# Edge counts in blocks of 16 destinations, the first residual bias as a matmul, and the last row tiles one by one

## The reference, cut to what matters

```python
n = 1250                                   # nodes, 768 features; 41250 edges, sorted by destination
loop = arange(n); dst = concat([edge_index[1], loop]); src = concat([edge_index[0], loop])
# layer 0: graph convolution
deg = segment_sum(ones, dst); norm = rsqrt(deg)[src] * rsqrt(deg)[dst]
x = layernorm(x + segment_sum((x @ W)[src] * norm[:, None], dst) + b)
# layer 1: two attention layers
def gat_conv(x, W, a_src, a_dst, bias, heads):
    xl = (x @ W).reshape(n, heads, -1)
    e = leaky_relu((xl * a_src).sum(-1)[src] + (xl * a_dst).sum(-1)[dst], 0.2)
    e = exp(e - segment_max(e, dst)[dst])
    alpha = e / segment_sum(e, dst)[dst]
    return segment_sum(xl[src] * alpha[..., None], dst).reshape(n, -1) + bias
h = gat_conv(x, W1, a_src1, a_dst1, b1, 4)                       # 4 heads of 256
h1 = relu(layer_norm(h, g1, be1)) + (x @ Wr1 + br1)              # "r1" is x @ Wr1 + br1
h = gat_conv(h1, W2, a_src2, a_dst2, b2, 1)
out = layernorm(x + layer_norm(h, g2, be2) + (h1 @ Wr2 + br2))
```

## Time and profile before

| what | us |
|---|---|
| three runs: lowest, median, highest | 953.65, 956.11, 956.56 |
| the profiled execution's own time | 956.15 |
| its span in the profile | 954.3 |
| PE, VectorE, ScalarE, GpSimd busy in the span | 852.7, 710.2, 300.8, 82.6 |

### The profile page before, as it was taken

How to read it: one execution, slowest core, us unless ns; L and a number is a source line. 1 busy time by engine, 2 the same in 40 slices (tenths; PEclk the granted TensorE clock), 3 DMA queues, 4 the chain that set the end, 5 groups by cost and what they waited for, 6 DMA issues and landing times.

```text
span 954.3 us, 12872 instructions
## 1 busy us (share of the span) xinstructions
PE 852.7 (89%) x4906; PEld 545.5 (57%) x4906; DVE 710.2 (74%) x1088; ACT 300.8 (32%) x451; POOL 82.6 (9%) x82
## 2 busy tenths in 40 slices
PE   2899999799799989965999988769899999999994
PEld 2566665466555434422888876658555656655552
DVE  6688888777746659794666698886796588965667
ACT  3133233500012101113577756635212207740000
POOL 2000000200000004441000010000110000000011
PEclk8899999899999989997999997889999999999998
DMA  7000001214121221313230011220102443222222
GB/s 274 1 1 1 2 1 67 84 40 156 75 121 45 67 79 67 121 66 94 91 105 28 28 50 56 67 71 23 45 27 96 157 179 101 84 83 67 67 68 95
DMA packets 23253, 70.32 MB, mean 74 GB/s; under 512 B 2614, under 2 KB 3338, under 8 KB 23070
## 3 DMA queue, kind: packets, MB, share of 16 engines
q1 hardware_dynamic: 21326, 61.80, 18.7%
q0 software_dynamic: 1872, 7.78, 2.4%
HBM read 49.26 MB, written 20.31 MB: 73 GB/s over the span
## 4 chain that ended last, share of the span: by engine, by line
issue 32%; PE 23%; DVE 21%; POOL 3%; ACT 2%; DMA 2%; POOLq 0%; DVEq 0%; ACTq 0%; SPq 0%
PE psum L787 12%; PE psum L608 9%; DVE arena L1186 7%; DVE arena L1287 2%; DVE arena L1291 2%; DVE arena L1310 1%; POOL arena L558 1%; DVE arena L1154 1%; ACT arena L922 1%; DMA arena<-as_scratch 1%; ACT arena L934 1%; DVE arena L1196 1%; POOL arena L542 1%; DVE arena L1318 1%; DVE arena L1181 1%
## 5 line engine op out<-in xcount | busy, mean ns | idle before, releaser
L608 PE MATMUL psum<-arena 128*128 128x512 f16 (+1 forms) x1080 | 227.6, 369 | 10.2 <-DVE arena L1006 9.2
L787 PE MATMUL psum<-arena 128*128 128x257 f32 x800 | 188.5, 399 | 31.1 <-ACT arena L922 22.1
L854 ACT ACTIVATE arena<-psum 128x320 f16<-128x320 f32 (+7 forms) x146 | 86.7, 629 | 380.6 <-PE psum L608 124.9
L787 PEld LDWEIGHTS psum<-arena 128*128 128x128 f32 x800 | 159.1, 200 | 59.0 <-issue 24.4
L608 PEld LDWEIGHTS psum<-arena 128*128 128x128 f16 (+1 forms) x1080 | 104.9, 99 | 118.1 <-DVE arena L1006 9.4
L760 PE MATMUL psum<-arena 128*128 128x512 f16 x960 | 159.3, 328 | 3.0 <-ACT arena L922 2.4
L760 PEld LDWEIGHTS psum<-arena 128*128 128x128 f16 x960 | 94.3, 98 | 65.8 <-ACT arena L922 2.8
L934 ACT ACTIVATE arena<-arena 128x640 f32<-128x640 f32 x160 | 119.6, 830 | 8.1 <-DVE arena L1291 7.0
L1186 DVE CUSTOM_DVE_ANT_0 arena<-arena 128x1280 bf16<-128x1280 bf16 x50 | 88.1, 1826 | 15.6 <-DMA arena<-as_scratch 11.8
L847 PE MATMUL psum<-arena 128*128 128x512 f16 x600 | 98.4, 326 | 0.0
L1287 DVE TENSOR_TENSOR arena<-arena 128x640 f32<-128x640 f32 x80 | 66.4, 830 | 37.0 <-ACT arena L934 36.2
(11 more groups left out here) (151 smaller groups left out, 608.5 us busy)
## 6 DMA issues: line engine op xcount, KB each, us to landing
arena<-in_L_gnn_W_dram SPq DMA_DIRECT2D x14, 384.0 KB, 5.7
r_scratch<-arena SPq DMA_DIRECT2D x10, 512.0 KB, 2.6
arena<-uv_scratch SPq DMA_DIRECT2D x16, 320.0 KB, 3.8
arena<-r_scratch SPq DMA_DIRECT2D x10, 512.0 KB, 3.6
x_scratch<-arena SPq DMA_DIRECT2D x10, 384.0 KB, 4.4
arena<-x_scratch SPq DMA_DIRECT2D x10, 384.0 KB, 3.6
r_scratch<-arena SPq DMA_DIRECT2D x10, 384.0 KB, 2.6
arena<-r_scratch SPq DMA_DIRECT2D x10, 384.0 KB, 4.0
```

The costliest lines, as they stand in the source:

```text
L608: ins = pe.matmul(o[:, a:b], part[:, k, ds(t * P, P)], w[:, k, a:b], start=(k == 0 and n == 0 and m == 0), stop=(k == kn - 1 and n == 1))
L787: last = pe.matmul(p_att[:, j, 0:HID + 1], pf[n % PSLOTS][:, j * P:(j + 1) * P], xl[ch % H][:, k, 0:HID + 1], start=(k == 0), stop=(k == T ...
L854: act.activation(out_, in_, ACT.Copy, scale=scale).then_inc(signal, 1)
```

## The change

Three edits are joined, and each is visible in the order of the instructions.

*Counting.* A block is 16 destinations, so there are 80 blocks, and a group is 6 edge tiles (one group per block, as with 32 and 10 before). The ring has 4 slots, PSUM 3. First and last edge tile of a block are packed in one word, read with one register load and taken apart by two register operations. The keys have two buffers and are shifted four blocks before they are wanted. x @ W is cut into 60 pieces that are spread over the blocks (`pieces_until`), none ahead of the first block; the six low parts of W0 come one by one between blocks 2 to 7. TAIL is 1.

*First residual.* The bias is split in two float16 rows (high and low part) and added by two matmuls of 512 columns that open each tile's sum. GpSimd makes the split once; its ten adds are gone, and ScalarE's output is stored as it is. The transposes of the sums and of the shifts stand inside the product's queue. ScalarE starts the exponentials before it takes the last tile out of PSUM.

*End.* Three pairs, then four single tiles. Of the last tile PE sums columns 512 to 768 first and then 0 to 512, VectorE takes the two parts as they come, and scales and stores in two halves.

```diff
-WD = 32
+WD = 16
-G = 10
+G = 6
+KSLOTS, CSLOTS = 4, 3
-TAIL = 3
+TAIL = 1
+PACK = 10
+W_LAG = 2
+def pieces_until(b):
+    return max(0, min(b + 1 - W_LAG, KD)) if b < SUBS else KD + (b + 1 - SUBS) * (T - 1) * KD // (NB - SUBS)
+PAIRS = 3
...
@@ SyncE @@
             for t in range(T):
-                if t == T - 1:
+                if t == T - 2:
                     sp.wait_ge(S["uv_rows"], 1)
...
-                sp.wait_ge(S["r1_sb"], t + 1)
+                sp.wait_ge(S["r1_read"], t + 1)
                 sp.dma_start(r1_d[t], r_st[t % 2]).then_inc(S[f"r1_out{t % 2}"], 16)
...
@@ GpSimd @@
+            pool.wait_ge(S["par_br1"], 16)
+            pool.wait_ge(S["br1_ok"], 2)
+            pool.tensor_scalar(par_rows[0:2, 3, :], par_rows[0:2, 3, :], WSCALE, None, ALU.mult).then_inc(S["br1_ok"], 1)
+            pool.wait_ge(S["br1_ok"], 3)
             pool.wait_ge(S["x1_ok"], T)
             param("par_b1", b1, 2)
...
+            pool.wait_ge(S["x1_tr"], T)
+            pool.wait_ge(S["x1_out"], 16 * T)
+            pool.tensor_copy(br1_parts, par_rows[0:2, 3, :]).then_inc(S["br1_ok"], 1)
+            pool.wait_ge(S["br1_ok"], 4)
+            for i in range(2):
+                cols = slice(i * HC // 2, (i + 1) * HC // 2)
+                pool.tensor_scalar(br1_less, br1_parts[:, cols], not_first[0:2], None, ALU.mult).then_inc(S["br1_ok"], 1)
+                pool.wait_ge(S["br1_ok"], 5 + 2 * i)
+                pool.tensor_tensor(br1_parts[:, cols], br1_less, par_rows[0:2, 3, cols], ALU.add).then_inc(S["br1_ok"], 1)
...
-            pool.wait_ge(S["par_br1"], 16)
-            for t in range(T):
-                pool.wait_ge(S["r1_read"], t + 3)
-                pool.tensor_tensor(r_st[t % 2], r_st[t % 2], par_rows[:, 3, :], ALU.add).then_inc(S["r1_sb"], 1)
-                if t == 3:
-                    for h in (2, 3):
-                        pool.wait_ge(S["max_ok"], 1)
...
+            for h in (2, 3):
+                pool.wait_ge(S["max_ok"], 1)
...
@@ TensorE @@
-            project_nodes(0, range(KD))
             pe.wait_ge(S["ranges_i"], 1)
...
-            for t in range(T):
-                for j in range(SUBS):
-                    count_block(t * SUBS + j)
-                    if j == 0 and t + 2 < T:
-                        transposes(t + 2)
-                    if t + 1 < T:
-                        project_nodes(t + 1, range(j * KD // SUBS, (j + 1) * KD // SUBS))
-                    if j == 2 and 1 <= t <= T - TAIL:
-                        degrees(t - 1)
+            for b in range(NB):
+                count_block(b)
+                t, j = b // SUBS, b % SUBS
+                if j == 0 and 1 <= t < T - 1:
+                    transposes(t + 1)
+                for q in range(pieces_until(b - 1) if b else 0, pieces_until(b)):
+                    project_nodes(q // KD, q % KD)
+                if j == SUBS - 1 and 1 <= t <= T - TAIL:
+                    degrees(t - 1)
...
+            for t in range(T):
+                o = p_x[t % 2]
+                if t < 2:
+                    pe.wait_ge(S["xl_read"], T + 1 + t)
+                else:
+                    pe.wait_ge(S["r1_read"], t - 1)
+                if t == T - 1:
+                    pe.wait_ge(S["uv_ok"], 1)
+                    pe.transpose(p_rows, uv.rearrange("p a t -> p (a t)"), ident).then_inc(S["uv_tr"], 1)
+                for a in (0, 512):
+                    pe.matmul(o[:, a:a + 512], ones_row, br1_parts[:, a:a + 512], start=True, stop=False)
+                product(o, (x1t_hi, x1t_lo), (wr1_hi, wr1_lo), t, KD, HC, range(KD // 2), True)
+                if t == 0:
+                    pe.wait_ge(S["as_ok"], 1)
+                    pe.transpose(p_rows, asd.rearrange("p a t -> p (a t)"), ident).then_inc(S["as_tr"], 1)
+                product(o, (x1t_hi, x1t_lo), (wr1_hi, wr1_lo), t, KD, HC, range(KD // 2, KD), True).then_inc(S["r1_done"], 1)
...
                     if k == 0 and ch:
                         pe.wait_ge(S["att_read"], (ch - 1) * C1 + j + 1)
+                    elif k == 0 and j in (2, 4):
+                        pe.wait_ge(S["r1_read"], T - 2 + j // 2)
...
+                for part in (((512, D), (0, 512)) if t == T - 1 else (None,)):
...
@@ ScalarE @@
-            act.wait_ge(S["r1_done"], T)
-            act.wait_ge(S["uv_ok"], 1)
-            act.wait_ge(S["neg_out"], 16)
+            act.wait_ge(S["xl_done"], T)
+            for t in range(T - 1):
+                r1_evict(t)
...
+            for n in range(ESLOTS):
+                exps(n)
+            r1_evict(T - 1)
+            for n in range(ESLOTS, H * T):
                 exps(n)
...
@@ VectorE @@
-                slot = b % 2
-                dve.reg_load(r0, range_i[0:1, b:b + 1])
-                dve.reg_load(r1, range_i[0:1, b + NB:b + NB + 1])
+                slot, keys = b % KSLOTS, key_s[b // SUBS % 2]
+                dve.reg_load(r0, packed[0:1, b:b + 1])
+                dve.reg_alu(r1, r0, PACK, ALU.logical_shift_right)
+                dve.reg_alu(r0, r0, (1 << PACK) - 1, ALU.bitwise_and)
...
+                one_hots(b)
+                if b < 2:
+                    xt_low(b)
+                elif b < W_LAG + KD:
+                    weights(0, [b - W_LAG])
+                if j == SUBS // 2 and t + 1 < T:
+                    dve.wait_ge(S["blk_done"], t * SUBS)
+                    dve.tensor_scalar(key_s[(t + 1) % 2], key_s[t % 2], float(-P), None, ALU.add).then_inc(S["key_shift"], 1)
+                if j == SUBS // 2 + 1 and 1 <= t < T - 1:
+                    xt_low(t + 1)
+                if j == SUBS // 2 + 2 and 1 <= t <= T - TAIL:
+                    low_counts(t - 1)
...
+                    j, left, right = js[0], slice(0, 512), slice(512, D)
+                    dve.scalar_tensor_tensor(y2[j][:, right], acc[:, j, right], rsum[:, j:j + 1], par_rows[:, 0, right],
+                                             ALU.mult, ALU.add).then_inc(S["att2_read"], 1)
+                    dve.wait_ge(S["att2_read"], read)
+                    spread(j, (1,), LAST_CUTS)
+                    dve.wait_ge(S["att2_done"], end + 1)
+                    dve.scalar_tensor_tensor(y2[j][:, left], acc[:, j, left], rsum[:, j:j + 1], par_rows[:, 0, left],
+                                             ALU.mult, ALU.add).then_inc(S["att2_read"], 1)
...
-            for c in range(T // C2 - 1):
-                finish(c, range(C2), c * 2)
-            for j in range(C2):
-                finish(T // C2 - 1, [j], 2 * (T // C2 - 1) + 2 * j)
+            for c in range(PAIRS):
+                finish(c * C2, (c + 1) * C2, c * 2, c + 1)
+            for i in range(T - PAIRS * C2):
+                t = PAIRS * C2 + i
+                finish(t, t + 1, 2 * PAIRS + 2 * i, PAIRS + 1 + i)
```

245 lines of the change are left out of this document (125 added, 120 removed).

## The result

| | before | after |
|---|---|---|
| median, lowest, highest (us) | 955.85, 953.65, 956.56 | 914.81, 913.32, 914.89 |
| executions | 4 | 4 |
| span in the profile | 954.3 | 911.5 |

The ratio is 0.9576 (95% interval 0.9564 to 0.9588): 41 us faster. The stages tell where the 9 us are; negative is faster, in us of the two profiled executions (956.15 and 913.32 us).

The account below looks back on a forecast made before the run. The prediction took TensorE to bound counting, and VectorE the first residual stage and the end. Its terms, -9 - 21 + 0.5 - 2.5 = -32, took 956.15 us to 924 us, with a range of 913 to 940.

Parts of the forecast that it names:

- the better case: Whole kernel: blocks at 0.77 us and a warm clock give about 912 us; chance 0.04.
- The counting term: Counting stage: earlier start and smaller blocks together save 9 us, from -15 to +5.
- the start: Start of counting: no wait behind the first weight product, so one-hots begin at 21.4 in place of 31.5 us.
- the block's price: Counting on PE: a block of 16 destinations costs 0.85 us, between 0.77 and 1.04.
- the loop's end: Counting block on PE: 0.29 us of the 1.77 us cadence go to it and the small last matmul.
- The rival of dear small matmuls: Counting on PE: at 107 ns per matmul a block costs 1.04 us, total 938 us; chance 0.15.
- VectorE's register loads: Counting: forecast hidden except one of 1.04 us at the start; rival, exposed at 80 blocks, 971 us, chance 0.04.
- The residual stage: First residual stage: without GpSimd's adds the maxima shorten and exponentials come earlier, -21 us, from -16 to -24.
- the warm clock: First 100 attention matmuls: a shorter pause ahead of them saves half of 2.9 us, counted as 1.4.
- The multiply: GpSimd's new multiply beside the first layer's last normalization on VectorE: +0.5 us, bounds 0 and 2.1.
- The end: End of the kernel: single last tiles and a split tile 9 save 2.5 us, from -1.5 to -3.

Follow-up runs that it names:

- open_by_loops: The changed kernel with self loops opening each block in one 160-column, 128-row matmul, without the zeros matmul and the 16-row closing one; 899.79 us.
- late_start: The changed kernel with the first weight product, its subtractions and the low parts of W0 put ahead of all counting blocks again; 914.63 us.
- bias_out: The changed kernel without the twenty bias matmuls of the first residual, so the bias is missing from its result; 914.80 us.
- both_better: The open_by_loops kernel with GpSimd's multiply of the bias rows moved from the first layer's last normalization to the bias split; 899.06 us.
- spare_adds: The changed kernel with ten GpSimd adds of 128x1024 given back, on rows that nobody reads; 930.19 us.

## Why the prediction was right, and where its sizes were off

What came is close to the better case of about 912 us (blocks at 0.77, a warm clock), to which the prediction gave a chance of 0.04.

**The counting term held two errors.** The forecast was -9: some 5.7 from the start and 0.3 a tile from the blocks. The end of counting moved by 17.2, and the runs split it the other way: 13.3 from the blocks, 3.9 from the start.

The step that failed is the block's price, 0.85 us with 0.77 as its lower bound. It took 0.29 us of the old cadence of 1.77 as the loop's end and the small matmul, after streaming 320 columns at the rate of 512-column matmuls. The weight loads say otherwise (timeline of before, then after):

```profile
161.39 1.36 PEld L636 LDWEIGHTS psum<-arena 128*128 128x128 f16 x10
```

```profile
45.85 0.45 PEld L665 LDWEIGHTS psum<-arena 128*128 128x128 f16 x6
```

Ten loads in 1.36 us, less one's own 0.10, are 0.140 from start to start; eleven matmuls make 1.54, and 0.23 are left. After it is (0.45 - 0.10) / 5 = 0.070, and a block 7 x 0.070 + 0.22 = 0.71. Of the 0.14 between 0.85 and 0.71, 0.08 is the margin that the prediction put on 0.77 in case small matmuls were dearer, and 0.06 is this loop's end. Over 72 blocks, 0.14 us each make 10.1; that is more than the miss, because the first tile ended 0.65 us later than forecast, the tiles' other work came out at 7.16 in place of 7.12 us, and the last tile lacked somewhat less. The bound was not a bound: the streaming that it took off came from a matmul of another size. And open_by_loops shows that of the 0.22 left, 0.21 is the small matmul's; "the loop's end", priced with it, is free.

The start was argued from a true row (the first product stood ahead of counting), and the first tile ended near its forecast (38.95 against 38.3). But its price did not ask what the old order gives with the new blocks, and late_start shows that the product may stay ahead of them. With blocks of 32 the new start gains 1.3 us, since VectorE is late there. With blocks of 16 it gains 2 to 4, and only by the waits for W0 row by row.

The rival of dear small matmuls (107 ns) did not come: 160 columns cost 70 ns. Dear is the change to few rows, which no row before the change shows by itself. The figure of the Trainium skill (TensorE: Matmul & The Clock Gate, Back-to-back issue gap) of about 81 ns at 128 columns in a sustained stream of loads and matmuls is above what this stream of loads and matmuls takes at 160; the trace decides. VectorE's register loads are hidden, as forecast: of its 18.3 us of idle time ahead of the first compare, 1.8 are issue, 1.67 of them ahead of the first block, where 1.04 were forecast (busy us, mean ns, idle before):

```profile
L1142 DVE TENSOR_TENSOR arena<-arena 128x768 f16<-128x768 int16 x80 | 44.3, 554 | 18.3 <-PE psum L665 15.2 <-issue 1.8
```

**The residual stage was right in mechanism and size.** -21 was forecast, -22.8 measured. Up to the first attention matmul it is -20.2 against -19.7. The mis-sized piece is the warm clock: half of 2.9 was counted, and 2.6 came, because a pause of 2.1 us in place of 5.2 left the clock at its full level. PE's tile 8 ended at 403.45 and the shifts were ready at 403.47, as close as forecast (418.1 and 418.5); bias_out shows which of the two bounds. That they still meet is luck. A tile took 8.41 us in place of 8.20, because the two bias matmuls have few rows, and VectorE waited 13.2 us for the score rows where it waited 11.8 before; counted from the projection's end, tile 8 came 1.6 and the shifts 1.2 us later than forecast.

**The multiply** beside the last normalization was priced at 0.5 (0 to 2.1). The normalization took 0.71 us more, and moving the multiply (both_better) takes that back; whether the whole time falls by as much, the medians can't tell. The Trainium skill (SBUF — State Buffer, Who interferes with whom) names tensor_scalar among the VectorE instructions that may contend with GpSimd; the trace agrees, with 1.40 in place of 0.69 us. It was not held until the multiply's end, though, as the maxima are by the adds.

**The end** was -2.5 by forecast, -2.7 in the trace, and 3.1 to 3.4 when taken back.

**Not settled:** the 1.0 us of the rest, most of it in the second layer's products, was not traced. Nor do the runs tell how much of the 13.3 us the deeper rings bring, or why PE does not load weights ahead where the number of rows changes.

## What to carry to other kernels

When a loop has two kinds of cost, take both from the rows of that loop: a rate borrowed from larger matmuls put part of the streaming into a "loop end" that does not shrink with the block. That and the margin on top hid most of the gain. Before pricing an earlier start, ask whether the next engine in line would be late anyway, and what the old order gives with the other edits; a run with the start alone and one without it answer it. And look at each matmul that uses few rows between full ones: filling its rows with zeros made it cheaper here (and brought time only where PE was the bound).

## What the runs showed of the hardware

- A matmul of 16 rows between matmuls of 128 rows cost 0.20 us more than one of 128 rows with the same 160 columns (block 0.70 against 0.50 us), and a pair with 2 rows and 512 columns 0.21 more than with 128 (tile 8.41 against 8.20). Weight loads are no longer (0.09 against 0.10 us), but at each change of the rows the load starts with its own matmul and not 0.07 us or more ahead of it, and 0.10 us are lost.
- A GpSimd multiply of 1024 elements takes 2.79 us on 2 partitions. An add of 512 elements on 2 partitions took 1.26 us, one of 1024 on 128 partitions 2.34 with no maximum beside it: about half the time for half the elements, so the partitions left out brought nothing that shows.
- GpSimd and VectorE hold each other. A maximum of 1.49 us that started inside an add took 3.62, and an add that takes 2.34 by itself took 3.17 where it started inside a maximum (363.83 in spare_adds). The multiply on 2 partitions held VectorE's single-input normalization too, but for 0.71 us only, and not until its own end.
